# A four-layer graph network: tables stored from 128 partitions, POOL's gathers written out, and the first half chunk taken ahead of the fill

## The chip, the cores and the metric

The kernel runs on one core of a Trainium2 chip. Its time is the device time of one execution in microseconds; several runs were made, and their median counts. The trace comes from one further execution under the hardware profiler. Engines go by the profile's names: PE (TensorE), DVE (VectorE), ACT (ScalarE), POOL (GpSimd), SP (SyncE, which here only starts DMAs).

## What is computed

A graph with N = 3125 nodes of 32 features and E = 53125 edges, sorted by destination node (every node has at least its loop). Four layers follow one another, each as `x = layernorm(x + layer(x))`. Cut to what matters:

```python
# layer 0: GAT with 4 heads, then a GRU cell on its sum
e = leaky_relu(el[src] + er[dst], 0.2)
alpha = softmax over the edges of one dst (e)
agg = segment_sum(feat[src] * alpha, dst)          # feat: N x 4 x 32
# layer 1: Chebyshev convolution of order 3 (two sums over edges), then GATv2
agg = segment_sum((x * Dinv)[src], dst)            # twice: cheb0, cheb1
e = leaky_relu(fsrc[src] + fdst[dst], 0.2); logits = e . attn; softmax; segment_sum
# layer 2: spline convolution, 4 x 4 tent basis of two edge attributes
msg = sum_k basis[:, k] * (x[src] @ w2[k]); out = segment_sum(msg, dst)
# layer 3: AGNN
alpha = beta * (x_norm[dst] . x_norm[src]); softmax; segment_sum(w * x[src], dst)
```

## The kernel before

**Layout.** Edges lie on 125 partitions (`NP`), 425 in a row (`T`); nodes lie on 125 partitions, 25 (`J`) each. `P` is 128, `SLOT` is 16, what a finished DMA adds to its semaphore, and `LS` is 5.

**Passes.** Five passes run over the edges: gat, cheb0, cheb1, gatv2 and agnn. Each takes the 425 columns in 17 chunks (`CH`) of 25 (`L`), in two buffers of `rows`. Every chunk needs the source node's row for each edge. Of its 25 columns, TensorE fetches 12 (gat) or 14 (`PE_COLS`) from a table that it holds, by products with one-hot matrices (L740); for that SP loads the source numbers to every partition (`load_sources`, L475), VectorE makes the one-hots (L1099), ScalarE the last of them (L921), and VectorE takes the products from PSUM with predicated copies (`take_half`, L1125). The other 13 or 11 columns POOL gathers by indirect DMA from a table in DRAM (`gather`, L600), which SP stored at the stage's start (`store_table`, L443). For each chunk SP loads the 25 columns of indices into `idx`; POOL waits for them and for the buffer (`rows_used`), adds two columns of ones into `fence` (L622, a `tensor_tensor` whose end the next fence waits for) and issues the gathers. VectorE then makes logits, running maxima and segmented scans, SP stores each scanned chunk, and at a pass's end POOL gathers 25 columns of node sums.

**Order on VectorE at a pass's start.** `begin_pass` (L1306) makes the parts of the table for TensorE and the one-hots of two chunks. Softmax passes then call `fill_edges` (L1293): it waits for the destination rows that were scattered into `starts_dram` and loaded back to `edges_d`, and spreads them over the edges with scans (64 in gatv2 and agnn, 8 in gat). `softmax_pass` (L1350) begins with three memsets (`start_scans`) and `take_half(0, 0, 0)`, which frees a part of PSUM for TensorE's next products.

**The spline stage.** TensorE multiplies each node's features with the weights (L879), ScalarE copies the products into `staged` in the layout of `tab_y` (L1040), five node columns a group, in two buffers, and SP stores each group of five columns as one DMA (L526): five stores of 2812 KB. ScalarE waits before group g for store g - 2. After the first store SP also stores the cell numbers that VectorE makes (L531), and loads them piece by piece into `idx` (L538), behind all stores of `tab_y`. POOL waits for the stores and the indices and gathers for each of 85 slots five rows of 128 floats (L600), in five buffers; from the sixth slot on there is a fence (L686) before each slot. VectorE works on each slot (L1696 to L1718), TensorE sums it (L785).

**What sets the order.** The orders on the engines are written out by hand. The helper `chunks` (L300) runs a pass's steps as two steps, a loop of 6 turns of two steps, and 3 steps; POOL's program uses it and a second loop for the spline, as SP's does.

## Time and profile before

| | before |
|---|---|
| runs | 2799.86, 2793.50, 2805.55 us; median 2799.86 |
| profiled execution | 2798.72 us |
| its span, first to last instruction | 2797.0 us |
| busy: PE, DVE, POOL, ACT | 69%, 64%, 68%, 31% of the span |
| mean granted TensorE clock | 0.831 of full |
| passes: POOL's first instruction to the end of its last row gather | gat 94.2 to 445.7, cheb0 579.9 to 843.7, cheb1 907.2 to 1170.0, gatv2 1271.3 to 1594.8, agnn 2430.9 to 2729.8 |
| spline: tab_y stored 1653.7 to 1766, gathers 1766.8 to 2368.8 | |

Busy shares are means over stages that differ. The times of the passes tell in which stage an instruction of a given start time lies. The profiled execution's time is 1.7 us longer than its span.

### The profile page before, as it was taken

Reading aid. Unit: us, or ns where it says so; the run is one execution under the profiler, and the core shown is the slowest. Engines: PE = TensorE matmul, PEld = TensorE weight load, DVE = VectorE, ACT = ScalarE, POOL = GpSimd, SP = SyncE. Lnnn points to the kernel's source line nnn. Section 1 sums busy time; section 2 is a strip of 40 time slices with the busy share of each in tenths; the row PEclk is TensorE's granted clock in tenths of the full one; section 3 lists DMA queues with packets and bytes.
Section 4 is the critical chain, followed back from the end, with each engine's and each line's share of the span. In section 5 each row is a group of like instructions: output and inputs, shape, how many; then the busy total and the mean of one; then the engine's idle time right before and its main releaser. Section 6 shows DMA issues by size and latency. Waiting matters only on the chain.

```text
span 2797.0 us, 52360 instructions
## 1 busy us (share of the span) xinstructions
PE 1938.7 (69%) x19915; PEld 1682.9 (60%) x19915; DVE 1784.3 (64%) x4803; ACT 879.6 (31%) x804; POOL 1915.2 (68%) x1825
## 2 busy tenths in 40 slices
PE   2577773669990999643988633487877788359990
PEld 2577773469990999633988611354544455259990
DVE  7499996155551455426878740477777777488785
ACT  0376774134440455310544322000000000125442
POOL 6788883357774777657888630588888887547873
PEclk6789886579995999856999855799999999679995
DMA  6243342123221322113222113211211111323321
GB/s 218 51 130 106 104 130 81 26 53 73 66 61 32 64 66 67 47 34 121 62 61 61 41 55 135 67 46 46 47 46 46 47 46 42 128 49 65 72 55 26
DMA packets 104646, 194.01 MB, mean 69 GB/s; under 512 B 52441, under 2 KB 71713, under 8 KB 100983
## 3 DMA queue, kind: packets, MB, share of 16 engines
q1 hardware_dynamic: 51528, 137.86, 13.3%
q0 software_dynamic: 53024, 54.88, 12.6%
q8 instruction: 62, 1.02, 0.2%
q14 instruction: 32, 0.26, 0.0%
HBM read 107.45 MB, written 85.19 MB: 69 GB/s over the span
## 4 chain that ended last, share of the span: by engine, by line
POOL 26%; issue 13%; DVE 10%; PE 10%; DMA 8%; ACT 1%; POOLq 0%; DVEq 0%; SPq 0%
POOL edges_d L600 16%; PE ps L740 8%; POOL rows L600 7%; DVE edges_d L1302 2%; DMA tab_y_dram<-edges_d 2%; POOL starts_dram L603 1%; POOL agg L600 1%; DMA idx<-cell_dram 1%; POOL fence L686 1%; DMA edges_d<-starts_dram 1%; DMA rows<-tab_fsrc_dram,idx 1%; PE ps L879 1%; DMA rows<-tab_x_dram,idx 1%; DVE bigT L1388 0%; DVE rows L1125 0%
## 5 line engine op out<-in xcount | busy, mean ns | idle before, releaser
L600 POOL DMA_INDIRECT edges_d<-tab_y_dram,idx x425 | 451.6, 1063 | 230.3 <-DMA idx<-cell_dram 113.6
L740 PE MATMUL ps<-nodes,edges_d 125*128 125x160 bf16 x7140 | 499.9, 234 | 101.9 <-ACT edges_d L921 98.4
L740 PEld LDWEIGHTS ps<-nodes,edges_d 125*128 125x128 bf16 x7140 | 498.4, 98 | 103.4 <-ACT edges_d L921 101.0
L785 PE MATMUL ps<-edges_d,scan 125*125 125x480 bf16 x1700 | 388.7, 390 | 142.2 <-DVE edges_d L1718 142.2
L600 POOL DMA_INDIRECT rows<-tab_cheb_dram,idx x374 | 407.0, 1088 | 109.1 <-issue 106.8
L740 PE MATMUL ps<-nodes,aggn 125*128 125x180 bf16 (+2 forms) x3372 | 377.9, 245 | 145.1 <-DVE rows L1125 145.1
L740 PE MATMUL ps<-nodes,agg 125*128 125x180 bf16 (+2 forms) x3564 | 342.6, 246 | 145.6 <-ACT aggn L921 80.7
L785 PEld LDWEIGHTS ps<-edges_d,scan 125*125 125x125 bf16 x1700 | 241.7, 145 | 289.7 <-DVE edges_d L1718 113.9
L1125 DVE COPY_PREDICATED rows<-picks,ps 125x192 f32<-125x192 uint16 (+4 forms) x850 | 342.7, 404 | 75.9 <-PE ps L740 23.3
L740 PEld LDWEIGHTS ps<-nodes,agg 125*128 125x128 bf16 x3564 | 290.1, 102 | 150.3 <-ACT aggn L921 81.4
L740 PEld LDWEIGHTS ps<-nodes,aggn 125*128 125x128 bf16 x3372 | 280.7, 102 | 149.5 <-issue 105.4
L600 POOL DMA_INDIRECT rows<-tab_dram,idx x221 | 272.9, 1235 | 64.7 <-issue 59.1
L600 POOL DMA_INDIRECT rows<-tab_fsrc_dram,idx x187 | 257.6, 1377 | 54.7 <-issue 52.4
L600 POOL DMA_INDIRECT rows<-tab_x_dram,idx x187 | 212.2, 1135 | 55.0 <-issue 52.4
L1696 DVE TENSOR_TENSOR edges_d<-edges_d 125x640 f32<-125x640 f32 x85 | 70.2, 826 | 247.1 <-DMA edges_d<-tab_y_dram,idx 247.1
L1049 ACT ACTIVATE agg<-prod 125x160 bf16<-125x160 f32 x85 | 28.6, 337 | 612.8 <-DVE prod L1707 612.8
L740 PE MATMUL ps<-nodes,smallT 125*128 125x160 bf16 (+1 forms) x2016 | 182.3, 236 | 0.0
L944 ACT ACTIVATE bigT<-rows 125x800 f32<-125x800 f32 x34 | 56.2, 1653 | 308.6 <-DVE rows L1125 308.6
L740 PEld LDWEIGHTS ps<-nodes,smallT 125*128 125x128 bf16 x2016 | 151.8, 99 | 0.0
L972 ACT ACTIVATE bigT<-rows 125x800 f32<-125x800 f32 x34 | 54.2, 1595 | 277.6 <-DVE idle L1475 151.0
L1692 DVE TENSOR_SCALAR scan<-nodes,codes 125x625 bf16<-125x625 f16 x340 | 133.1, 408 | 0.0
L603 POOL DMA_INDIRECT starts_dram<-scat,start_i x75 | 76.5, 1019 | 81.4 <-DVE scat L1760 28.1
(330 smaller groups left out, 3123.9 us busy)
## 6 DMA issues: line engine op xcount, KB each, us to landing
src<-srcT_dram SPq DMA_DIRECT2D x68, 427.2 KB
scan_dram<-scan SPq DMA_DIRECT2D x17, 1700.0 KB
scan_dram<-scan SPq DMA_DIRECT2D x34, 425.0 KB
tab_y_dram<-edges_d SPq DMA_DIRECT2D x5, 2812.5 KB
scanD_dram<-scan SPq DMA_DIRECT2D x34, 400.0 KB
edges_d<-starts_dram SPq DMA_DIRECT2D x2, 3408.0 KB, 20.1
starts_dram<-scan SPq DMA_DIRECT2D x2, 3400.0 KB, 15.3
edges_d<-tab_y_dram,idx POOLq DMA_INDIRECT x425, 2.6
```

The costliest lines, as they stand in the source:

```text
L600: pool.indirect_dma_start(o, None, table, bass.IndirectOffsetOnAxis(index, 0)).then_inc(s, SLOT)
L603: pool.indirect_dma_start(table, bass.IndirectOffsetOnAxis(index, 0), rows_, None, bounds_check=last, oob_is_err=False).then_inc(scattered ...
L686: pool.tensor_tensor(fence[:, 0:1], ones[:, 0:1], ones[:, 1:2], ALU.add)\
L740: ins = pe.matmul(columns_ps[:, i, 0:PICKS * w], hots_[b][lot][:, i * NP:i * NP + P], parts_[:, part, at:at + PICKS * w], start=(lot == 0 ...
L785: ins = pe.matmul(ps[0:NP, lot, 0:PICKS * 3 * D], lot_hots[c][:, t, lot, :], picked[c][:, t, :, :].rearrange("p k c -> p (k c)"), start=(b ...
L944: nc.scalar.activation(z[b][:, at:at + D, :], r[:, :, 0:D].rearrange("p t f -> p f t"), ACT.Copy).then_inc(rows_flipped, 1)
L972: nc.scalar.activation(z[b], rows[0:NP, b, 0:L * D].rearrange("p (t c) -> p c t", c=D), ACT.Copy).then_inc(rows_used, 1)
L1049: nc.scalar.activation(parts[:, c, :, 0:D], prod[:, c * LS:(c + 1) * LS, :], ACT.Copy)\
L1125: ins = vec.copy_predicated(to[:, cols[0]:cols[-1] + 1, 0:w], over(picks[:, b, pick, cols[0]:cols[-1] + 1], w), columns_ps[0:NP, cols[0]:c ...
L1302: ins = vec.tensor_tensor_scan(ed[:, t0:t1, c], same[:, t0:t1], ed[:, t0:t1, c], ed[:, t0 - 1, c:c + 1] if i else 0.0, ALU.mult, ALU.add)
L1692: vec.tensor_scalar(lot_hots[c][:, t, :, :].rearrange("p l c -> p (l c)"), nodes16[:, 0:LOTS * NP], codes[:, c, t:t + 1], None, ALU.is_equal)
L1696: vec.tensor_tensor(slot, slot, over(basis[:, bass.ds(t0 + c * LS, LS), :], D), ALU.mult)\
```

## The change

DRAM tables get 128 × 25 rows in place of 3125, and every table store, the stores of `tab_y` and the loads of source numbers go from or to 128 partitions instead of 125. POOL's program has no loops any more; the fences and their semaphore are gone; the indices are no longer loaded chunk by chunk: all source numbers lie in `src_i`, loaded once at the start, and the cell numbers in `cell_i`, where VectorE writes them. `fill_edges` is called inside `softmax_pass`, behind the first `take_half`. Three memsets clear partitions 96 to 127 of the buffers.

```diff
-        tab_cheb_dram = [dram("tab_cheb0_dram", (N, D)), dram("tab_cheb1_dram", (N, D))]
-        tab_y_dram = dram("tab_y_dram", (N * CELLS * CELLS, CORNERS * D))
-        cell_dram = dram("cell_dram", (E,), I32)
+        tab_cheb_dram = [dram("tab_cheb0_dram", (P * J, D)), dram("tab_cheb1_dram", (P * J, D))]
+        tab_y_dram = dram("tab_y_dram", (P * J * CELLS * CELLS, CORNERS * D))
...
-        idx = sb("idx", [P, 2, L], I32)
+        src_i = sb("src_i", [P, T], I32)
...
-        attr = sb("attr", [NP, T, 2])
+        attr = sb("attr", [P, T, 2])
+        cell_i = attr[:, :, :].rearrange("p t d -> p (t d)")[:, 0:T].bitcast(I32)
...
-        staged = edges_d[0:NP, 0:2 * LS * YROW].rearrange("p (b j c) -> p b j c", b=2, j=LS)
+        staged = edges_d[:, 0:2 * LS * YROW].rearrange("p (b j c) -> p b j c", b=2, j=LS)
...
+                    if a is lambda_max_row:
+                        sp.wait_ge(tails_cleared, 1)
+                        sp.dma_start(src_i[0:NP, :], src_grid).then_inc(src_loaded, SLOT)
...
-                        sp.dma_start(src16[0:NP, b, 0:n * NP], srcT_dram[bass.ds(t0 + L - n, n), :]
-                                     .rearrange("t p -> (t p)").partition_broadcast(NP)).then_inc(src16_in[b], SLOT)
+                        sp.dma_start(src16[:, b, 0:n * NP], srcT_dram[bass.ds(t0 + L - n, n), :]
+                                     .rearrange("t p -> (t p)").partition_broadcast(P)).then_inc(src16_in[b], SLOT)
 
                     def step(k, b, t0):
-                        if gathered[b].n or k >= 2:
-                            sp.wait_ge(rows_in[b], gathered[b].at())
-                        sp.dma_start(idx[0:NP, b, :], src_grid[:, bass.ds(t0, L)]).then_inc(idx_in[b], SLOT)
-                        gathered[b].up(SLOT * (L - PE_COLS[name]))
                         if k < CH - 1:
                             load_sources(k + 1, 1 - b, t0 + L)
...
-                store_table(tab_cheb_dram[0], tabf[0:NP, 0:J * D])
+                store_table(tab_cheb_dram[0], tabf[:, 0:J * D])
...
-                    if g == 0:
-                        sp.wait_ge(cells_made, 1)
-                        sp.dma_start(cell_grid, cell_i).then_inc(cells_stored, SLOT)
-                sp.wait_ge(cells_stored, SLOT)
...
-                load_indices(0, True)
-                with sp.Fori(0, CH - 1) as turn:
-                    for c in slot_n:
-                        c.enter(turn, SLOT * LS)
-                    load_indices(turn * L + L, False)
...
-                    def step(k, b, t0):
-                        pool.wait_ge(idx_in[b], loaded[b].up(SLOT))
+                    for k in range(CH):
                         if k >= 2:
                             pool.wait_ge(rows_used, used.up())
-
-                        if fences.n:
-                            pool.wait_ge(fence_done, fences.at())
-                        pool.tensor_tensor(fence[:, b:b + 1], ones[:, 0:1], ones[:, 1:2], ALU.add)\
-                            .then_inc(fence_done, 1)
-                        fences.up()
                         for t in range(L - PE_COLS[name]):
-                            gather(rows[:, b, t * width:(t + 1) * width], table, idx[:, b, t:t + 1], rows_in[b])
-
-                    chunks(pool, [(loaded[0], SLOT), (loaded[1], SLOT), (used, 2), (fences, 2)], step)
+                            gather(rows[:, k % 2, t * width:(t + 1) * width], table,
+                                   src_i[:, k * L + t:k * L + t + 1], rows_in[k % 2])
...
-                for c in range(SLOTS):
-                    pool.wait_ge(slot_idx_in[c], idx_n[c].up(SLOT))
-                    gather_slot(c)
-                with pool.Fori(0, CH - 1) as turn:
...
+                pool.wait_ge(cells_made, 1)
+                for n in range(CH * SLOTS):
+                    if n >= SLOTS:
+                        pool.wait_ge(slot_used, n - SLOTS + 1)
                     for t in range(LS):
-                        gather(slots[:, c, t * CORNERS * D:(t + 1) * CORNERS * D], tab_y_dram,
-                               idx[:, 0, c * LS + t:c * LS + t + 1], slot_in[c])
+                        gather(slots[:, n % SLOTS, t * CORNERS * D:(t + 1) * CORNERS * D], tab_y_dram,
+                               cell_i[:, n * LS + t:n * LS + t + 1], slot_in[n % SLOTS])
...
+                vec.memset(src_i[96:P, :].bitcast(F32), 0.0)
+                vec.memset(attr[96:P, :, :], 0.0).then_inc(tails_cleared, 1)
+                vec.memset(tab[96:P, :, :], 0.0)
...
-                def softmax_pass(name, logits):
+                def softmax_pass(name, logits, fill_width, fill_at):
                     table, width, scan_dram, C, heads = PASSES[name]
                     z, keep, n = scan_views(name)
                     start_scans(name)
                     take_half(0, 0, 0, name)
+                    fill_edges(fill_width, fill_at)
...
                 begin_pass("gat", tab[0:NP, :, 0:D + H], 1)
-                fill_edges(H, D + H)
```

Three places of the engines' orders follow; a row is a line of the kernel, the operation, the written and read names and the shape, with what it waits for.

On VectorE, at the start of gatv2, before (`edges_d` holds the destination rows, `picks` and `ps` belong to `take_half`; the scans are named SCALAR_TENSOR_TENSOR here):

```order
L1109 TENSOR_SCALAR picks<-pick_of 125x70
L1299 COPY edges_d<-first_row 125x32
L1302 SCALAR_TENSOR_TENSOR edges_d<-same,edges_d 125x212 x32
L1302 SCALAR_TENSOR_TENSOR edges_d<-same,edges_d 125x213 x32
L1334 MEMSET bigT 125x33
L1335 MEMSET bigT 125x33
L1336 MEMSET mrun 125x4
L1124 MEMSET idle 125x1
L1125 COPY_PREDICATED rows<-picks,ps 125x192
```

and after the change (its line numbers are those of the changed kernel):

```order
L1054 TENSOR_SCALAR picks<-pick_of 125x70
L1282 MEMSET bigT 125x33
L1283 MEMSET bigT 125x33
L1284 MEMSET mrun 125x4
L1069 MEMSET idle 125x1
L1070 COPY_PREDICATED rows<-picks,ps 125x192
...
L1070 COPY_PREDICATED rows<-picks,ps 125x192
L1247 COPY edges_d<-first_row 125x32
L1250 SCALAR_TENSOR_TENSOR edges_d<-same,edges_d 125x212 x32
L1250 SCALAR_TENSOR_TENSOR edges_d<-same,edges_d 125x213 x32
```

The copies of the first half chunk (five instructions, of which the first and the last stand here; the second half's stay behind) and the memsets now come ahead of the 65 instructions of the fill.

On POOL, in the spline stage, before (the end of the first slots, the loop's entry and its first slot):

```order
L600 DMA edges_d<-tab_y_dram,idx 128x128 [waits slot_idx_in3]
L600 DMA edges_d<-tab_y_dram,idx 128x128 x4
L600 DMA edges_d<-tab_y_dram,idx 128x128 [waits slot_idx_in4]
L600 DMA edges_d<-tab_y_dram,idx 128x128 x4
L677 UNCONDITIONAL_BRANCH
L677 ISA
L684 ISA [waits slot_idx_in0]
L685 REGISTER_ALU [waits slot_used]
L686 TENSOR_TENSOR fence<-ones 128x1 [waits fence_done]
L600 DMA edges_d<-tab_y_dram,idx 128x128 x5
```

and after:

```order
L628 IOTA nodes 125x625
L573 DMA edges_d<-tab_y_dram,attr 128x128 [waits cells_made,products_stored1,products_stored0]
L573 DMA edges_d<-tab_y_dram,attr 128x128 x24
L573 DMA edges_d<-tab_y_dram,attr 128x128 [waits slot_used]
L573 DMA edges_d<-tab_y_dram,attr 128x128 x4
L573 DMA edges_d<-tab_y_dram,attr 128x128 [waits slot_used]
L573 DMA edges_d<-tab_y_dram,attr 128x128 x4
```

The branch, the fences and the waits for index loads are gone; the wait for `slot_used` stands at each slot's first gather, and `attr` is the memory that holds the cell numbers.

On SP, around the stores of `tab_y`, before:

```order
L526 DMA tab_y_dram<-edges_d 125x5760 [waits group_copied]
L531 DMA cell_dram<-aggn 125x425 [waits cells_made]
L526 DMA tab_y_dram<-edges_d 125x5760 [waits group_copied] x4
L538 DMA idx<-cell_dram 125x5 [waits cells_stored]
L538 DMA idx<-cell_dram 125x5 x4
```

and after:

```order
L473 DMA src<-srcT_dram 128x1750 [waits last_hot_ready]
L486 DMA scan_dram<-scan 128x850 [waits rows_turned] x4
L520 DMA tab_y_dram<-edges_d 128x5760 [waits group_copied] x5
L441 DMA tab_x_dram<-tab 128x825 [waits vec_for_sync]
L441 DMA tab_xn_dram<-scat 128x800 [waits vec_for_sync]
```

The store and the loads of the cell numbers are gone, and the five stores come from 128 partitions.

## Rows read from the trace of the kernel before

**Rows 1.** The page: span, busy time and its share by engine

```profile
span 2797.0 us, 52360 instructions
PE 1938.7 (69%) x19915; PEld 1682.9 (60%) x19915; DVE 1784.3 (64%) x4803; ACT 879.6 (31%) x804; POOL 1915.2 (68%) x1825
```

**Rows 2.** Stretches: length, busy us by engine (PE to POOL), clock, DMA share, GB/s

```profile
58.00:72.00 14.00, 0.58 (x2) 0.49 (x2) 11.79 (x29) 0.22 (x1) 8.41 (x8) 0.50 1.02 423
570.00:579.00 9.00, 0.00 (x0) 0.00 (x0) 2.91 (x4) 0.00 (x0) 0.00 (x0) 0.50 0.32 96
1733.00:1764.00 31.00, 0.00 (x0) 0.00 (x0) 0.00 (x0) 0.00 (x0) 0.00 (x0) 0.50 0.32 136
1766.00:2370.00 604.00, 474.32 (x2082) 296.29 (x2083) 444.52 (x1040) 28.28 (x84) 483.97 (x505) 0.92 0.19 47
```

**Rows 3.** Chain that ended last, 1640 to 1790: start, us, what

```profile
1653.70 25.08 DMA tab_y_dram<-edges_d
1688.37 34.87 DMA tab_y_dram<-edges_d
1731.91 34.08 DMA idx<-cell_dram
```

**Rows 4.** ACT's timeline, spline stage: start, us, instruction [idle before, releaser]

```profile
1663.38 1.32 ACT L1040 ACTIVATE edges_d<-ps 125x288 f32<-125x288 f32 x4 [0.39 <-PE ps L879]
1678.80 2.53 ACT L1040 ACTIVATE edges_d<-ps 125x288 f32<-125x288 f32 x8 [14.10 <-DMA tab_y_dram<-edges_d]
```

**Rows 5.** Line L459, two stores of 3400 KB: their landing

```profile
DMA to landing us min/median/max: 11.2/15.3/19.4
```

**Rows 6.** Spline: two groups of the page, then two lines' instructions

```profile
L600 POOL DMA_INDIRECT edges_d<-tab_y_dram,idx x425 | 451.6, 1063 | 230.3 <-DMA idx<-cell_dram 113.6
L1696 DVE TENSOR_TENSOR edges_d<-edges_d 125x640 f32<-125x640 f32 x85 | 70.2, 826 | 247.1 <-DMA edges_d<-tab_y_dram,idx 247.1
...
L600 POOL DMA_INDIRECT edges_d<-tab_y_dram,idx x425: 940/964/1587, 1766.8 to 2367.7; - x142
...
L686 POOL TENSOR_TENSOR fence<-ones x80: 200/400/662, 1800.6 to 2361.2; 128x1 f32<-128x1 f32 x80
```

**Rows 7.** POOL's timeline inside the spline stage, around two fences

```profile
1998.82 1.14 POOL L600 DMA_INDIRECT edges_d<-tab_y_dram,idx  x1 [0.30 <-issue]
1999.98 0.20 POOL L686 TENSOR_TENSOR fence<-ones 128x1 f32<-128x1 f32 x1
2000.33 0.96 POOL L600 DMA_INDIRECT edges_d<-tab_y_dram,idx  x1 [0.15 <-issue]
...
2006.54 0.59 POOL L686 TENSOR_TENSOR fence<-ones 128x1 f32<-128x1 f32 x1
```

**Rows 8.** Timelines at the Chebyshev passes (SP, DVE, POOL, ACT, POOL)

```profile
568.38 0.28 SPq L443 DMA_DIRECT2D tab_cheb_dram<-tab  x1
579.69 2.53 DVE L1099 TENSOR_SCALAR edges_d<-src,lot_f 125x1754 bf16<-125x1754 f16 x4 [6.67 <-DMA src<-srcT_dram]
579.92 0.49 POOL L622 TENSOR_TENSOR fence<-ones 128x1 f32<-128x1 f32 x1 [56.21 <-issue]
845.13 1.54 ACT L972 ACTIVATE bigT<-rows 125x800 f32<-125x800 f32 x1 [7.88 <-DMA rows<-tab_cheb_dram,idx]
907.15 0.50 POOL L622 TENSOR_TENSOR fence<-ones 128x1 f32<-128x1 f32 x1 [16.40 <-issue]
```

**Rows 9.** Timelines at gatv2 and agnn, and the page's group L1125

```profile
1282.67 0.18 DVE L1299 COPY edges_d<-first_row 125x32 f32<-125x32 f32 x1 [23.70 <-DMA edges_d<-starts_dram]
1319.14 0.56 PE L740 MATMUL ps<-nodes,aggn 125*128 125x160 bf16 x3 [43.82 <-DVE rows L1125]
1329.69 0.19 POOL L622 TENSOR_TENSOR fence<-ones 128x1 f32<-128x1 f32 x1 [6.18 <-DVE bigT L1388]
2488.67 0.19 POOL L622 TENSOR_TENSOR fence<-ones 128x1 f32<-128x1 f32 x1 [25.49 <-DVE bigT L1388]
L1125 DVE COPY_PREDICATED rows<-picks,ps 125x192 f32<-125x192 uint16 (+4 forms) x850 | 342.7, 404 | 75.9 <-PE ps L740 23.3
```

91 lines of the change are left out of this document (28 added, 63 removed).

## The prediction

> **What bounds the kernel now.** I read the page first. No engine fills the span: TensorE is busy 69%, VectorE 64%, POOL 68% [rows 1], so the stages have different limits, and a change is worth what the last wait of its stage is worth. Then I read the chain of work that ended last, to find stretches in which no engine works. The largest lies between the second layer's attention pass (gatv2) and the third layer's spline convolution: two stores of the table tab_y, 25.08 and 34.87 us, and then an index load that takes 34.08 us [rows 3]. That load is small; it stands behind the last tab_y store in SP's queue. POOL's first spline gather starts at 1766.8 and had waited 113.6 us for it [rows 6].
>
> In the Chebyshev passes the start is late: the table is stored at 568.38, VectorE gets its source numbers at 579.69 after idling 6.67, POOL starts at 579.92, and the last chunk still waits 7.88 us for gathered rows [rows 8]. So POOL's stream, shifted by its late start, ends last there.
>
> In gatv2 and agnn VectorE fills the rows of the destination table (64 scans, some 34 us) before it takes the first half chunk, and TensorE stands 43.82 us until then [rows 9]. Afterwards POOL's stream is again what the others wait for, so TensorE's idle time is worth little.
>
> **The change, part by part.**
>
> *tab_y stores.* Before, store 0 goes at 1653.70 and lands at 1678.78. ScalarE, which writes the staging buffers, waits 14.10 us for it at the third group [rows 4], and so once for each later group. A store of 128 partitions moves 2880 KB; at 423 GB/s that is 6.8 us. What lies around the transfer I take from the starts stores: 3400 KB are 8.0 us at that rate and the first lands after 11.2 [rows 5], so 3.2 us are added: 10.0 us a store. ScalarE makes a group of five tiles in 9.57 us (1678.80 to 1688.37) [rows 3, 4]; a store of 10.0 us is back before its buffer is wanted, two groups later. So ScalarE no longer waits. It ended the second group at 1663.38 + 1.32 = 1664.70 [rows 4], and three groups later stands at about 1694.5 (two of them hold an extra copy, so about 9.9 each). The last store lands at 1704.5 and the first gather comes 0.7 later, about 1705, for 1766.8 before: **−61.8 us**. VectorE has nothing to do in the stretch from 1733 [rows 2], so the cell numbers that POOL's gathers also need are no bound. Bounds: if ScalarE's groups come at 7.2 us (its own busy time), −69; if a store needs 17 us because several buffers, other queues or the memory slow it, −55.
>
> *The fence in the spline.* 80 fences of 400 ns median go [rows 6]. What one costs POOL is its spacing against that of two gathers. In the quiet case the gather ends at 1999.96, the fence runs 0.20 and the next gather starts at 2000.33: 0.37 between the ends where 0.30 is normal [rows 7], so 0.07 each, 5.6 us in all. From the sums: 424 spacings take 600.9 us (1766.8 to 2367.7), a plain spacing is 1.063 + 0.30 = 1.363 [rows 6, 7], 344 of them are 468.9, and the 80 with a fence come to 1.65 each: 0.287 more, 23 us in all. The difference between the ends is that half of the fences are stretched to 0.59 to 0.66 beside VectorE's work [rows 7]. Whether that stretching goes with them or falls on the gathers is open; a gather is stretched too (0.96 to 1.14). I take **−12**, near the middle, with 5.6 and 23 as ends. POOL stays the bound: of 604 us TensorE is busy 474.3 and VectorE 444.5 [rows 2], 5.6 and 5.2 us of the 7.07 per slot.
>
> The Trainium skill bears on this ("SBUF — State Buffer", on the port pair that VectorE and GpSimd share): the pair is locked for a whole instruction, and a gather's descriptors cannot be written until VectorE's operation ends. By that rule the stretching belongs to VectorE's operations and not to the fence, the gathers would inherit it, and the sum would be smaller by about 6 us. The stretched fence of 0.59 beside one of 0.20 agrees with a lock; no row here shows who inherits it.
>
> *Chebyshev passes.* The table store of 400 KB needs about 1 us of transfer at 423 GB/s and the 3.2 us around it, so POOL may start at about 572.3 in place of 579.9; its first fence and the step behind it (0.64) go, and 15 fences at 0.07. That is 7.6 + 0.6 + 1.0 = 9.2 on POOL's side. On VectorE's side the idle 6.67 vanishes, since the 427 KB of source numbers (1 us at 423 GB/s, behind 1 us of table, and the 3.2) land at about 573.6 where VectorE came free at 573.0, 6.67 before 579.69; the second load, 1 us behind, is then hidden too. POOL's rows end last by the 7.88 [rows 8]; when POOL gains 9.2 and VectorE about 7, the wait shrinks and POOL still ends last. **−9** for cheb0, and **−9** for cheb1, whose first fence stands in the same way at 907.15 after 16.40 idle [rows 8]. Ends −6.5 and −10 each.
>
> *The fill behind the first half chunk.* In gatv2 the five predicated copies of the half chunk (5 × 0.404 [rows 9], 2.0) and three small memsets (0.2, an estimate) move from behind the fill into idle time ahead of it, since VectorE waits there 23.70 us for the destination rows [rows 9]. POOL waits 6.18 us for chunk 0 to be used, so it gains those 2.2, and 15 × 0.07 for fences: **−3.3**. In agnn POOL waits 25.49 [rows 9]: the same 2.2, 1.1 of fences, and, an estimate, 1.3 of a shorter wait of POOL on chunk 1: **−4.6**. TensorE's 43.8 us idle are filled with chunk 1's products, which nobody waited for. If POOL were not the bound behind it, chunk 1's second half would be worth up to 5 us in each; if the fill's scans find TensorE's results no earlier, nothing.
>
> *gat* I leave almost as it is: **−0.4**, its 17 fences at 0.07 (1.2) a third on the path (0 to −3).
>
> *The start.* Three memsets are added on VectorE ahead of its wait for the destination numbers: **+0.2** (0 to 1). The load of all source numbers (212 KB) stands ahead of some weights and is hidden by the gathers of destination rows that VectorE waits for afterwards; if it is not hidden it costs 212 KB at the 136 GB/s of five engines [rows 2], 1.6.
>
> *Indices.* 170 small index loads go, with their issue time on SP and their latency; in the steady stream they were early, so nothing beyond the above.
>
> *Sum.* −61.8 − 12 − 9 − 9 − 3.3 − 4.6 − 0.4 + 0.2 = −99.9. The profiled span of 2797.0 becomes 2697.1, the profiled execution's 2798.7 becomes 2698.8. The median of the runs shown is 1.1 above the profiled execution, so I say **2699 us**.
>
> **The rivals.** About 0.5% (14 us) is what a measurement of this kernel can tell from no change.
>
> *Contention stays and moves (0.15).* The wider loads of source numbers (one per chunk, 16 engines for 1 us in place of five for 3) and the bare stream of gathers are stretched more: every plain spacing in the spline goes up by 0.09 to 1.45, as in the slowest stretches. Then the spline saves 5.6 and loses 38; total about −62 or 2737. For it: plain gathers range from 0.94 to 1.59 [rows 6]. Against: the extremes are few (median 0.964).
>
> *The wide store does not spread (0.04).* If tab_y and the other tables still go over five engines, only the fences, the order of SP's queue (no index load behind the last store is needed, but POOL waits for the store itself) and the fill are left: −12 − 2 − 2 − 3.3 − 4.6, about −24: 2775. Against: stores and loads of 128 partitions on the same queue show share 1.02.
>
> *More than forecast (0.18).* ScalarE's groups come faster, because TensorE, busy without gaps, is granted a higher clock than 0.50 in that stretch (windows: 0.50 while it idles), and the fences' full 23 us come back: −69 − 23 − 10 − 10 − 6 − 6 = −124, or 2675.
>
> *Slower (0.03).* POOL's program is now written out: 1394 gathers in a row where a loop of one turn's length stood. If fetching them cost POOL 0.08 us or more a gather ((100 + 14) / 1394), the gain would be gone; at 0.12 the time is 2866. Against: a turn of the spline loop already holds 25 gathers in a straight run, and they go at 0.94 + 0.30 at their quickest [rows 6, 7], which is the issue time of any gather here. The Trainium skill ("Runtime: NRT & Kernel Launch", section "Instruction fetch mechanics") says that crossing a fetched block is mostly hidden and that a taken branch is what stalls; by that rule the change gains a little there.
>
> *The forecast* itself has 0.6.
>
> **How the numbers follow.** The forecast's own range adds its ends: −69 − 23 − 13 for the best (2684 to 2690 if not all at once) and −55 − 5.6 − 13 − 5 for the worst (2720): 2682 to 2720. Eight in ten: down to 2670, which takes in the larger gain, and up to 2726, which takes in a part of the contention case; the rest of it, the unspread store and the slower case are left out. Faster by over 0.5% in all cases but the slower one and mishaps between: 0.96; same 0.015; slower 0.025.
>
> **What the profile after would show.** Windows of a lone tab_y store with a share near 1.0 and above 400 GB/s; ScalarE without waits on tab_y in the spline stage; first spline gather near 1705 less what the stages ahead gained (about 22 us), so near 1683; gather spacing 1.36 or less and a slot of 6.9 us; POOL's first cheb0 gather 4 us behind the table store; TensorE without the 43.8 us in gatv2 and agnn. The prediction is wrong if the tab_y stores take over 15 us each, if gathers stretch beyond 1.4 spacing, or if POOL shows gaps between gathers above 0.30 that nothing releases.

## The result, and the profile after

The changed kernel takes 2660.85 us (median of four runs, 2658.53 to 2662.79) against 2800.41 (2793.50 to 2805.55). The ratio is 0.9503, 95% interval 0.9481 to 0.9525: 139.6 us less. The forecast was 2699, and its range ended at 2670. The profiled execution took 2661.16, its span is 2658.2, which is 138.8 less than that of [rows 1].

The page of the changed kernel, with the groups that answer to [rows 6] (gathers are line L573 here, and L1643 is what was L1696):

```profile
span 2658.2 us, 51172 instructions
PE 1904.6 (72%) x19915; PEld 1661.4 (63%) x19915; DVE 1801.5 (68%) x4806; ACT 879.6 (33%) x804; POOL 1846.9 (69%) x1659
...
L573 POOL DMA_INDIRECT edges_d<-tab_y_dram,attr x425 | 431.9, 1016 | 180.7 <-issue 129.2
...
L1643 DVE TENSOR_TENSOR edges_d<-edges_d 125x640 f32<-125x640 f32 x85 | 71.2, 837 | 131.1 <-DMA edges_d<-tab_y_dram,attr 131.1
```

The gathers of the spline take 1016 ns on average where they took 1063, VectorE waits for them 131.1 us where it waited 247.1, and the fences' group is gone.

I cut the two traces at POOL's gathers, whose first start and last end mark each stage. "Sums" are the 25 gathers of node sums that follow each pass. Times in us; the last column is how far the changed kernel had pulled ahead by the event, and in brackets what the stage itself added.

| event | before | after | ahead by (stage) |
|---|---|---|---|
| sums of gat begin | 491.6 | 489.0 | 2.6 (2.6) |
| sums of cheb0 begin | 859.8 | 850.0 | 9.8 (7.2) |
| sums of cheb1 begin | 1186.0 | 1171.3 | 14.7 (4.9) |
| sums of gatv2 begin | 1621.4 | 1594.2 | 27.2 (12.5) |
| first spline gather | 1766.8 | 1677.5 | 89.3 (62.1) |
| last spline gather ends | 2368.8 | 2238.5 | 130.3 (41.0) |
| sums of agnn begin | 2754.6 | 2615.7 | 138.9 (8.6) |

The stores of tab_y gave what was forecast (62.1 for 61.8). The spline stage gave 41.0 where 12 were forecast, gatv2 12.5 for 3.3, agnn 8.6 for 4.6, the Chebyshev passes together 12.1 for 18, and all ahead of them 2.6 for 0.2.

Two stretches of the changed kernel (columns as in [rows 2]): around the cheb0 table store, and while a tab_y store is under way.

```profile
565.00:572.00 7.00, 0.00 (x0) 0.00 (x0) 6.46 (x9) 0.00 (x0) 2.73 (x3) 0.50 0.68 191
1660.00:1666.00 6.00, 6.00 (x8) 1.82 (x7) 0.00 (x0) 4.14 (x13) 0.00 (x0) 0.50 1.01 430
```

The tab_y store now has a DMA share of 1.01 and 430 GB/s, where it had 0.32 and 136 [rows 2]. Its five stores land after (line L520):

```profile
DMA to landing us min/median/max: 8.2/8.2/8.7
```

That is 8.2 us a store; I had worked out 10.0. ScalarE's timeline in the same stage, and POOL's first spline gather:

```profile
1657.04 1.32 ACT L985 ACTIVATE edges_d<-ps 125x288 f32<-125x288 f32 x4 [0.39 <-PE ps L824]
1667.64 1.32 ACT L985 ACTIVATE edges_d<-ps 125x288 f32<-125x288 f32 x4 [0.51 <-PE ps L824]
...
1677.45 0.96 POOL L573 DMA_INDIRECT edges_d<-tab_y_dram,attr  x1 [51.52 <-DMA tab_y_dram<-edges_d]
```

ScalarE's waits on tab_y [rows 4] are gone; it waits 0.39 to 0.51 for TensorE's products, and now and then 1.7 to 2.2. POOL begins 8.5 us after ScalarE's last copy ends (1668.96), one landing and the issue.

POOL's timeline inside the spline stage, one slot of five gathers and the next slot's first:

```profile
1904.25 0.94 POOL L573 DMA_INDIRECT edges_d<-tab_y_dram,attr  x1 [0.30 <-issue]
1905.50 1.25 POOL L573 DMA_INDIRECT edges_d<-tab_y_dram,attr  x1 [0.30 <-issue]
1907.05 0.94 POOL L573 DMA_INDIRECT edges_d<-tab_y_dram,attr  x1 [0.30 <-issue]
1908.30 0.94 POOL L573 DMA_INDIRECT edges_d<-tab_y_dram,attr  x1 [0.30 <-issue]
1909.55 1.08 POOL L573 DMA_INDIRECT edges_d<-tab_y_dram,attr  x1 [0.30 <-issue]
1910.94 0.94 POOL L573 DMA_INDIRECT edges_d<-tab_y_dram,attr  x1 [0.30 <-issue]
```

This slot takes 6.69 us (1904.25 to 1910.94). Three of its gathers are unstretched, one takes 1.25 and one 1.08. The stage has 85 slots in 561 us, 6.6 each, for 7.07 before.

The start of cheb0 (SP's table store, POOL's first gather, TensorE's first product, POOL's first gather of chunk 2):

```profile
565.75 0.33 SPq L441 DMA_DIRECT2D tab_cheb_dram<-tab  x1
...
568.66 0.94 POOL L573 DMA_INDIRECT rows<-tab_cheb_dram,src_i  x1 [47.65 <-DMA tab_cheb_dram<-tab]
...
577.01 23.17 PE L685 MATMUL ps<-nodes,edges_d 125*128 125x160 bf16 x298 [31.29 <-ACT edges_d L866]
...
600.59 0.94 POOL L573 DMA_INDIRECT rows<-tab_cheb_dram,src_i  x1 [4.18 <-ACT bigT L917]
```

POOL starts 2.9 us after the store, where it had taken 11.5 [rows 8]. But then it waits 4.18 us at chunk 2 for a buffer. TensorE starts 11.3 us after the store, where it took 17.4 in the trace before, whose store goes at 568.38 [rows 8]:

```profile
585.76 26.42 PE L740 MATMUL ps<-nodes,edges_d 125*128 125x160 bf16 x347 [37.41 <-ACT edges_d L921]
```

The fill in gatv2 (VectorE's copy and scans, TensorE's wait behind it, POOL's gathers beside it):

```profile
1267.88 0.29 DVE L1247 COPY edges_d<-first_row 125x32 f32<-125x32 f32 x1 [24.46 <-DMA edges_d<-starts_dram]
1268.20 11.96 DVE L1250 TENSOR_TENSOR_SCAN edges_d<-same,edges_d 125x212 f32<-125x212 f32 x24
...
1306.43 0.58 PE L685 MATMUL ps<-nodes,aggn 125*128 125x160 bf16 x3 [50.64 <-DVE rows L1070]
...
1275.83 9.09 POOL L573 DMA_INDIRECT rows<-tab_fsrc_dram,src_i  x1 [0.30 <-issue]
1288.14 14.65 POOL L573 DMA_INDIRECT rows<-tab_fsrc_dram,src_i  x1 [0.31 <-issue]
...
1313.11 0.96 POOL L573 DMA_INDIRECT rows<-tab_fsrc_dram,src_i  x1 [3.71 <-DVE bigT L1337]
```

TensorE still stands 50.64 us, for 43.82 before [rows 9], and two of POOL's gathers take 9.09 and 14.65 us while the scans run (9.10 and 14.66 in the trace before).

### The profile page after: what moved, and what is told of

Its sections match the earlier page's. It is cut to its first block, busy times and chain, and to the rows that moved or that the text cites. A ratio compares the mean times of both kernels' runs of the same rounds, so it can differ in the third digit from the quotient of the medians.

```text
span 2658.2 us, 51172 instructions
## 1 busy us (share of the span) xinstructions
PE 1904.6 (72%) x19915; PEld 1661.4 (63%) x19915; DVE 1801.5 (68%) x4806; ACT 879.6 (33%) x804; POOL 1846.9 (69%) x1659
## 4 chain that ended last, share of the span: by engine, by line
POOL 37%; issue 13%; DVE 7%; PE 4%; DMA 3%; ACT 1%; POOLq 0%; DVEq 0%; ACTq 0%
POOL rows L573 19%; POOL edges_d L573 16%; DVE edges_d L1250 2%; PE ps L685 2%; PE ps L824 2%; POOL starts_dram L576 1%; POOL agg L573 1%; DMA edges_d<-starts_dram 1%; DMA tab_y_dram<-edges_d 0%; ACT edges_d L985 0%; DVE bigT L1293 0%; PE ps L809 0%; PE ps L805 0%; PE ps L730 0%; DMA local<-scan_dram,mend_get_i 0%
## 5 line engine op out<-in xcount | busy, mean ns | idle before, releaser
L573 POOL DMA_INDIRECT edges_d<-tab_y_dram,attr x425 | 431.9, 1016 | 180.7 <-issue 129.2
L573 POOL DMA_INDIRECT rows<-tab_cheb_dram,src_i x374 | 409.7, 1095 | 177.4 <-issue 112.5
L730 PE MATMUL ps<-edges_d,scan 125*125 125x480 bf16 x1700 | 364.1, 371 | 108.6 <-DVE edges_d L1665 108.6
L685 PE MATMUL ps<-nodes,agg 125*128 125x180 bf16 (+2 forms) x3564 | 337.3, 244 | 112.9 <-ACT aggn L866 58.6
L730 PEld LDWEIGHTS ps<-edges_d,scan 125*125 125x125 bf16 x1700 | 227.9, 137 | 245.9 <-DVE edges_d L1665 113.0
L573 POOL DMA_INDIRECT rows<-tab_dram,src_i x221 | 277.0, 1253 | 67.5 <-issue 66.4
L573 POOL DMA_INDIRECT rows<-tab_fsrc_dram,src_i x187 | 250.5, 1340 | 60.4 <-issue 56.7
L573 POOL DMA_INDIRECT rows<-tab_x_dram,src_i x187 | 228.3, 1221 | 61.9 <-issue 56.7
L1069 DVE MEMSET idle<- 125x1 f32 x850 | 50.1, 59 | 171.6 <-PE ps L685 129.9
L1643 DVE TENSOR_TENSOR edges_d<-edges_d 125x640 f32<-125x640 f32 x85 | 71.2, 837 | 131.1 <-DMA edges_d<-tab_y_dram,attr 131.1
L889 ACT ACTIVATE bigT<-rows 125x800 f32<-125x800 f32 x34 | 56.3, 1656 | 310.4 <-DVE rows L1070 310.4
L917 ACT ACTIVATE bigT<-rows 125x800 f32<-125x800 f32 x34 | 54.2, 1595 | 277.3 <-DVE idle L1424 151.6
L1639 DVE TENSOR_SCALAR scan<-nodes,codes 125x625 bf16<-125x625 f16 x340 | 142.9, 437 | 0.0
```

What stands on the lines that cost most here:

```text
L573: pool.indirect_dma_start(o, None, table, bass.IndirectOffsetOnAxis(index, 0)).then_inc(s, SLOT)
L685: ins = pe.matmul(columns_ps[:, i, 0:PICKS * w], hots_[b][lot][:, i * NP:i * NP + P], parts_[:, part, at:at + PICKS * w], start=(lot == 0 ...
L730: ins = pe.matmul(ps[0:NP, lot, 0:PICKS * 3 * D], lot_hots[c][:, t, lot, :], picked[c][:, t, :, :].rearrange("p k c -> p (k c)"), start=(b ...
L889: nc.scalar.activation(z[b][:, at:at + D, :], r[:, :, 0:D].rearrange("p t f -> p f t"), ACT.Copy).then_inc(rows_flipped, 1)
L917: nc.scalar.activation(z[b], rows[0:NP, b, 0:L * D].rearrange("p (t c) -> p c t", c=D), ACT.Copy).then_inc(rows_used, 1)
L1069: vec.memset(idle[:, half * 8 + pick:half * 8 + pick + 1], 0.0)
```

## The experiments

All are against the changed kernel (2660.9 us), but for the first two, which are the kernel before with parts of the change. Given are medians and the ratio to the kernel before, measured beside each on the same chip (2797.5 to 2804.6 us). Lengths of stages come from the one profiled execution of each kernel and not from the median (in e3 and e9 it was the quickest of four). A pass's stream is POOL's first row gather to the end of its last.

### Which part gives what

**e1_tables.** The kernel before, and all table stores from 128 partitions:

```diff
-                store_table(tab_cheb_dram[0], tabf[0:NP, 0:J * D])
+                store_table(tab_cheb_dram[0], tabf[:, 0:J * D])
...
-        staged = edges_d[0:NP, 0:2 * LS * YROW].rearrange("p (b j c) -> p b j c", b=2, j=LS)
+        staged = edges_d[:, 0:2 * LS * YROW].rearrange("p (b j c) -> p b j c", b=2, j=LS)
```

> The kernel before with one part of the change: all table stores, those of tab_y too, from 128 partitions. Source numbers, indices, fences, loops and the fill's place are as before. If the stores alone give what the trace of after suggests, the wait for tab_y falls by 62 us and the two Chebyshev passes start 8 us earlier each on POOL's side, of which the narrow load of source numbers takes back some: together 62 to 78 us, a time of 2722 to 2738. If the wide store gains only together with the removal of the cell index load, the gain stays under 40 us.

2733.69 us, ratio 0.9743 (0.9723 to 0.9762): 71 less. Its first spline gather stands at 1702.8, so the wide store alone is worth the tab_y term; the removal of the cell index load isn't needed for it.

**e2_no_pool.** As e1, with the wide loads of source numbers and the fill behind the first half chunk; POOL's program as before.

> The change without its POOL part: wide stores, wide loads of source numbers and the fill behind the first half chunk are in; loops, fences and index loads stay as before. Theory (fences, or what comes with them, cost far more than 0.07 us each): 2715 to 2730, so that POOL's part is worth 55 to 70 us, and a spline slot stays at 7.07 us. Rival (wide loads or the stores relieve the gathers): the spline stage is already shorter here, a slot is at 6.6 us, and the time is under 2700.

2721.97 us, 0.9714 (0.9697 to 0.9730). The spline stage takes 600.4 us, as before (602.1). So the spline's gain, and 61 us in all, come with POOL's part (fences, loops and index loads).

**e5_narrow_src.** Source numbers loaded to 125 partitions again:

```diff
-                        sp.dma_start(src16[:, b, 0:n * NP], srcT_dram[bass.ds(t0 + L - n, n), :]
-                                     .rearrange("t p -> (t p)").partition_broadcast(P)).then_inc(src16_in[b], SLOT)
+                        sp.dma_start(src16[0:NP, b, 0:n * NP], srcT_dram[bass.ds(t0 + L - n, n), :]
+                                     .rearrange("t p -> (t p)").partition_broadcast(NP)).then_inc(src16_in[b], SLOT)
```

> The changed kernel with the source numbers loaded to 125 partitions, as before. Theory (in the Chebyshev passes TensorE, not POOL, sets the end once POOL starts early, so that what counts there is when the first source numbers land): 2.5 us more in each Chebyshev pass and 2 us more ahead of gat, 7 to 8 us in all, 2668 to 2670. Rival (POOL's stream still ends last): no change in the two passes, 2661 to 2664. Second rival (the wide loads stretch the gathers of the other passes): the time falls.

2672.75 us, 0.9553 (0.9531 to 0.9576), 12 more, above every range of the expectation. In the trace cheb0 and cheb1 are longer by 3.2 us each, with POOL's start as early as in the changed kernel (569.2 and 568.7). TensorE's first product comes at 579.24 for 577.01. The rest are short waits of TensorE of 0.3 to 0.9 us. In cheb0 TensorE takes 252.5 us from its first product to the last of the 17 chunks, 251.2 in the changed kernel and 252.1 in the kernel before, whenever POOL started. So the passes' end follows TensorE, and not POOL. The two passes hold 6.4 of the 12 us; of the others 3.1 lie in the spline, whose instructions are the same, and 1.9 in gatv2. The 2 us ahead of gat did not come (sums of gat at 489.3 for 489.0).

### What the fences cost

**e3_spline_fence.** The 80 fences of the spline put back into the straight program:

```diff
                         pool.wait_ge(slot_used, n - SLOTS + 1)
+                        if fences.n:
+                            pool.wait_ge(fence_done, fences.at())
+                        pool.tensor_tensor(fence[:, 0:1], ones[:, 0:1], ones[:, 1:2], ALU.add).then_inc(fence_done, 1)
+                        fences.up()
```

> The changed kernel with the 80 fences of the spline stage put back; no index loads, no loops. Theory (the fence is what made a slot 7.07 us): the spline stage grows by 35 to 41 us and the time is 2696 to 2702. Rival (the index loads and the loop did it): a fence adds only its quiet cost of 0.07 to 0.3 us, 6 to 23 us in all, and the time is 2667 to 2684.

2707.07 us, 0.9662 (0.9639 to 0.9685): 46 more, and in the trace the spline stage is 601.6 us, 40.6 longer, 0.51 a fence. Its loops and index loads are gone, and the stage is as long as before: with the fences in place they cost nothing there. The size has a margin: the stage takes 600.4 to 602.1 in five traces with 80 fences, and 561.0 to 571.3 in eight without a POOL operation in their places, so 80 fences cost 29 to 41 us. POOL's timeline, two fences a slot apart, with VectorE's L1672 ahead of each:

```profile
1903.36 1.41 DVE L1672 TENSOR_TENSOR edges_d<-agg,pick_bits 125x1200 int32<-125x1200 int32 x1
1905.60 0.21 POOL L641 TENSOR_TENSOR fence<-ones 128x1 f32<-128x1 f32 x1
1905.96 0.96 POOL L576 DMA_INDIRECT edges_d<-tab_y_dram,attr  x1 [0.15 <-POOL fence L641]
...
1911.32 1.41 DVE L1672 TENSOR_TENSOR edges_d<-agg,pick_bits 125x1200 int32<-125x1200 int32 x1
1912.19 0.60 POOL L641 TENSOR_TENSOR fence<-ones 128x1 f32<-128x1 f32 x1
1912.93 0.97 POOL L576 DMA_INDIRECT edges_d<-tab_y_dram,attr  x1
1914.21 1.40 POOL L576 DMA_INDIRECT edges_d<-tab_y_dram,attr  x1 [0.30 <-issue]
```

The pattern is that of [rows 7]: a fence of 0.21, and one of 0.60 with a gather of 1.40 behind it. The trace says which are stretched. All 40 stretched fences (0.59 and more) start while VectorE runs L1672, an operation of 1.41 us that reads two operands from SBUF, and end 0.05 us after it; all 40 short ones start while VectorE is idle. In the trace before it is the same, 40 and 40, with L1718.

**e8_two_fences.** Two fences at each of those places.

> The changed kernel with two fences at each place of the spline stage. Theory A (each fence has a price of its own, 0.5 us): the stage grows by another 35 to 41 us against one fence, about 642 us, and the time is 2740. Theory B (a slot of POOL's stream and VectorE's work on it lock into a pattern, and the first fence moved them into a worse one): the second fence costs its quiet 0.2 to 0.35 us a slot, 16 to 28 us, or the stage is even shorter than with one; 600 to 628 us.

2743.33 us, 0.9801 (0.9781 to 0.9821); the stage takes 640.0 us, 38.4 more than with one. A second fence costs as much as the first, and theory B falls. But the price is not the stretching of the fences themselves: 159 of these 160 take their short 0.2 us and start while VectorE is idle, and all 160 together take 32.5 us, as the 80 did (32.4). The further 38.4 us are on the gathers, whose mean rises from 1062 to 1138 ns, and in the gaps between. Why the gathers pay for it when the fences don't, no run here takes apart.

**e7_spline_memset** and **e11_one_operand.** In the fences' places a memset, and a copy:

```diff
+                        pool.memset(fence[:, 0:1], 1.0).then_inc(fence_done, 1)
...
+                        pool.tensor_copy(fence[:, 0:1], ones[:, 0:1]).then_inc(fence_done, 1)
```

> The changed kernel with a memset of one column on POOL in each place where the spline stage had a fence: an operation of the same place and semaphore that reads nothing. The 80 fences put back made the stage 40.6 us longer. Theory 1 (any POOL operation between gathers costs this, since it must wait for the memory port that VectorE holds, and delays the gathers behind it): 35 to 41 us more than the changed kernel, about 2700. Theory 2 (it is the reading of two operands from the memory): 5 to 15 us more, 2666 to 2676.

> The changed kernel with a copy of one column (one operand read from the memory, one written) in each place where the spline stage had a fence. The fence, which reads two operands, cost 40.6 us there, and a memset, which reads none, 9.0. If it is the second operand that makes the fence wait for VectorE's port: about 9 to 14 us, 2670 to 2675. If any reading costs it: 30 to 41 us, 2691 to 2702.

The memset: 2673.08 us, 0.9552 (0.9534 to 0.9569), stage 570.0, 9 us more than in the changed kernel, but within the 561.0 to 571.3 of the kernels with nothing there: a cost of its own isn't shown. The copy: 2695.27 us, 0.9642 (0.9624 to 0.9661), stage 600.4, 39.4 more, all but the fence's price. POOL's timelines, the memset first, with VectorE's L1672 ahead of it:

```profile
1901.29 1.41 DVE L1672 TENSOR_TENSOR edges_d<-agg,pick_bits 125x1200 int32<-125x1200 int32 x1
1902.14 0.11 POOL L641 MEMSET fence<- 128x1 f32 x1
1902.44 1.08 POOL L576 DMA_INDIRECT edges_d<-tab_y_dram,attr  x1 [0.19 <-POOL fence L641]
```

```profile
1905.32 0.20 POOL L641 COPY fence<-ones 128x1 f32<-128x1 f32 x1
1905.68 0.98 POOL L576 DMA_INDIRECT edges_d<-tab_y_dram,attr  x1 [0.15 <-POOL fence L641]
...
1911.85 0.60 POOL L641 COPY fence<-ones 128x1 f32<-128x1 f32 x1
1912.61 0.98 POOL L576 DMA_INDIRECT edges_d<-tab_y_dram,attr  x1 [0.16 <-POOL fence L641]
1913.90 1.43 POOL L576 DMA_INDIRECT edges_d<-tab_y_dram,attr  x1 [0.30 <-issue]
```

The memset is never stretched (80 of them take 118 ns on average, 125 at most), though 68 of the 80 start inside L1672. The copy alternates between 0.20 and 0.60 with a stretched gather behind the latter, just as the fence does; its 41 stretched ones all start inside L1672. So it isn't the second operand, and not any operation either. What is stretched is a POOL operation that reads SBUF while VectorE runs a two-operand operation. That the reading does it, and nothing else in which a memset differs from a copy, rests on these three operations.

**e6_pass_fence** and **e13_all_fences.** The 85 fences of the passes put back, and all 165.

> The changed kernel with the 85 fences of the five passes put back. Theory (a fence costs POOL 0.5 us where VectorE is dense and POOL's stream sets the end, and nothing where TensorE does): gatv2 7 to 9 us, agnn 2 to 5, gat 0 to 2, the Chebyshev passes 0; 10 to 15 us more, 2671 to 2676. Rival (loops and index loads were the cost of these passes): under 4 us more.

> The changed kernel with all 165 fences put back, its program still without loops and index loads. Theory (fences are all of POOL's part): 2718 to 2724, as the kernel with everything but POOL's part (2722). Rival (loops and index loads have a share of their own): 2705 or less.

e6: 2682.78 us, 0.9574 (0.9555 to 0.9593), 22 more. Chunks 2 to 16 take 262.1 us in gatv2 for 254.7, and 245.0 in agnn for 235.7; gat's stream is 10.3 longer without moving its sums (489.2), and the Chebyshev passes get no longer. Against the expectation agnn lost more than gatv2, and 10 us lie in the spline, whose code was not touched (below). e13: 2709.16 us, 0.9679 (0.9660 to 0.9699), 48 more, between the two expectations. There the same chunks take 257.7 and 239.7. Only agnn's difference is clear of what the same code does by itself: its stream takes 298.8 (e6) and 295.8 (e13) with fences and 289.3 to 293.1 in six kernels whose agnn has none, so its 17 fences cost 2.7 to 9.5 us. gatv2's takes 318.1 and 313.8 with fences, and 308.7 to 323.1 in the same six: a price of the fences there isn't shown. Nor do the parts add up, 46 (e3) and 22 (e6) against 48 for both. e13 stays 13 us below e2. Of POOL's 61 us fences are 48. The spans of e13 and e2 differ by only 7.0 us, of which 6.2 lie between the sums of cheb1 and of gatv2 and 2.5 in agnn's stage; whether that is the loops, the index loads or the scatter shown by e12 below was not told apart. The kernel before without fences wasn't run.

### The fill

**e4_fill_first.** The fill ahead of the first half chunk again:

```diff
+                    fill_edges(fill_width, fill_at)
...
                     take_half(0, 0, 0, name)
-                    fill_edges(fill_width, fill_at)
```

> The changed kernel with the fill of destination rows ahead of the first half chunk again, as before, in the three softmax passes. Theory (the place of the fill is worth the 2.2 us of the moved copies in gatv2 and agnn each, and the rest of the gain of these passes is the fences'): 3 to 7 us more, 2664 to 2668. Rival (TensorE's 43.8 idle us matter later in the pass): 12 us or more.

2672.99 us, 0.9531 (0.9515 to 0.9547): 12 more, the rival's number. From POOL's first gather to that of chunk 2 gatv2 takes 57.9 us for 55.9, and agnn 56.3 for 54.2: the moved copies' 2.0 us, as forecast. The rest lies in the chunks behind (259.4 for 254.7, 240.2 for 235.7) and in the spline (565.1 for 561.0), where the instructions are the same. In gatv2 and the spline that is within what the same code does by itself (e12); agnn's stream, 296.5, is not (289.3 to 293.1), so the rival isn't excluded there. Nor is the 2.0 seen everywhere: between e1 and e2, which move the fill with the fences in place, gatv2's falls from 58.8 to 56.3 while agnn's stays (58.5 and 58.6).

**e12_same_again.** The changed kernel once more, for how far a stage of the same code repeats.

> The changed kernel itself once more. If the lengths of gatv2, spline and agnn are properties of the code, they come out as in its first profile, 310.6, 561.0 and 289.9 us from POOL's first row gather to the end of the last, within 1 us, and the median at 2659 to 2663. If they depend on how the two engines happen to lock into each other, they differ by several us (the same code took 308.8 to 323.1 for gatv2 in the kernels with changed neighbours).

2663.11 us, 0.9519 (0.9506 to 0.9532). gatv2 took 312.3 us for 310.6, spline 564.5 for 561.0, agnn 289.3 for 289.9. So a stage repeats within 3.5 us in the same kernel, and from kernel to kernel the untouched spline took 561.0 to 571.3, the untouched stream of gatv2 308.7 to 323.1 (e8, where only the spline differs) and that of agnn 289.3 to 293.1. Differences of a stage within these ranges are no evidence, gatv2's least of all.

**e9_split_fill.** The fill cut at column 50, the second part after chunk 1:

```diff
-        FILLS = [(0, T // 2), (T // 2, T)]
+        FILLS = [(0, 2 * L), (2 * L, T)]
...
-                                 (kept, 2), (used, 2), (flipped, 2), (scanned, 2)] + HOT_COUNTS, step)
+                                 (kept, 2), (used, 2), (flipped, 2), (scanned, 2)] + HOT_COUNTS, step,
+                           lambda: fill_edges(fill_width, fill_at, 1))
```

> The changed kernel, and the fill cut in two at column 50 in place of 212: the first 50 columns are loaded and filled ahead of chunk 0, the other 375 after chunk 1. In gatv2 and agnn VectorE can begin chunk 0 some 34 us earlier (the load of 50 columns lands about 6 us earlier and 28 us of scans come later). Theory (POOL waits for chunk 0 to be used and is then the bound, VectorE idles 25 us a pass in all): 15 to 30 us less per pass, 2600 to 2630. Rival (VectorE becomes the bound at once, or gathers blocked beside the fill eat it): only the earlier load of 6 us a pass, 2645 to 2652.

2676.25 us, 0.9556 (0.9535 to 0.9577), 15 more, where 9 to 61 less were expected. VectorE did begin chunk 0 early, and POOL's chunk 2 begins 34.9 us after its first gather for 55.9. But beside the second part of the fill POOL loses it again:

```profile
1313.03 1.46 POOL L573 DMA_INDIRECT rows<-tab_fsrc_dram,src_i  x1 [0.30 <-issue]
1314.79 22.00 POOL L573 DMA_INDIRECT rows<-tab_fsrc_dram,src_i  x1 [0.30 <-issue]
1337.10 1.49 POOL L573 DMA_INDIRECT rows<-tab_fsrc_dram,src_i  x1 [0.30 <-issue]
```

One gather takes 22.00 us. POOL reaches chunk 4 of gatv2 92.0 us after its first gather, for 90.2 in the changed kernel, where the fill blocked two gathers for 23.7 together and POOL waited only 3.71 more. Ahead of chunk 0 that blocking costs nothing: in e11, with the same gatv2, no gather beside the fill took over 1.3, and chunk 2 began after 55.7 us for 55.9. Behind chunk 1 it falls into time in which POOL has buffers to fill. Where the 15 us are isn't shown by this: in the profiled execution gatv2's whole stage is 3.6 us shorter, agnn's 5.7 longer, and 7.8 lie in the untouched spline.

**e10_uneven_fill.** `FILLS = [(0, 130), (130, T)]`, all of it ahead of chunk 0.

> The changed kernel with the fill's two loads cut at column 130 in place of 212, all of it still ahead of chunk 0. The first load is 3.2 us shorter, so the fill starts and ends 3.2 us earlier, and POOL waits 3.7 and 5.2 us for chunk 0 in gatv2 and agnn. Theory: 3 us less in each, 2654 to 2656. Rival (a slot or chunk pattern of VectorE and POOL swallows or doubles such shifts, as between kernels with the same code in these stages, whose gatv2 took 307.7 to 315.6 us): anything from 2648 to 2670, and the gain at the second fill's end is seen while the pass's end is not earlier.

2654.63 us, 0.9491 (0.9474 to 0.9508), 6.2 and 8.5 less than the two measurements of the changed kernel. VectorE's scans in gatv2, and POOL's first gather of chunk 2:

```profile
1262.09 10.47 DVE L1250 TENSOR_TENSOR_SCAN edges_d<-same,edges_d 125x130 f32<-125x130 f32 x32
1273.57 23.32 DVE L1250 TENSOR_TENSOR_SCAN edges_d<-same,edges_d 125x295 f32<-125x295 f32 x32 [1.00 <-DMA edges_d<-starts_dram]
...
1308.01 0.97 POOL L573 DMA_INDIRECT rows<-tab_fsrc_dram,src_i  x1 [2.46 <-DVE bigT L1337]
```

The second part waits 1.00 us for its rows, so the two loads and the scans are near balance at 130; no other cut was run. Chunk 2 begins 53.9 us after the first gather for 55.9, and in agnn 51.6 for 54.2. Of this agnn keeps nothing: its chunks behind take 238.4 for 235.7, and the stream ends after 290.0 for 289.9, which was the expectation's rival. In the trace gat gave 1.7 us and gatv2's stage 2.4, the latter within its scatter.

**e14_best.** e10 with the last store of tab_y in two parts, three node columns and then two.

> The changed kernel with the fill's loads cut at column 130 (which gave 6 to 8 us) and the last store of tab_y cut in two, three node columns and then two, so that after the last product only 1152 KB are to be stored: 2.7 us at the rate of the wide stores in place of 6.8, the first three columns being under way before. If the last store's landing is what POOL's first spline gather waits for: 3 to 4 us less than with the cut fill alone, 2649 to 2652. If the stores queue up behind each other, no gain: 2653 to 2656.

2654.85 us (2643.99 to 2658.69), 0.9484 (0.9464 to 0.9505). POOL's first spline gather comes 5.1 us after ScalarE's last copy for 8.5, so the stage gained the 3.4; the total doesn't show it beyond its spread. Its fill is that of e10, and yet chunk 2 begins 58.0 and 56.1 us after the first gather for 53.9 and 51.6, with gathers of 10.05 and 18.57 us beside gatv2's scans; the agnn stream still takes only 288.8. So the start of chunk 2 does not by itself set a pass's end. Both medians lie 6 us or more below those of the changed kernel (2660.85 and 2663.11); between the two nothing is decided.

## Why the prediction was wrong

**The step that failed** is *the fence in the spline*, and with it the fences in agnn. I bounded it by 0.07 us (a quiet fence) and by 0.287, the sum's excess at fences over a plain spacing, and took −12 of at most −23. It is 40.6 for 80 fences (e3; 29 to 41 by the other traces), and again 38.4 for a second set (e8). The upper bound was no bound: I took the plain spacing of the kernel with fences as what a gather costs anyway, 1.363. Part of that stretching came with the fences. Without them a spacing is 1.32, so 344 plain spacings gave back some 15 us beside what the 80 gave. A price read as "spacing with, less spacing without" must take the "without" from a stretch that has none; the trace before had such stretches only in other stages.

The other reading of that part, that the stretching belongs to VectorE's operations and the gathers would inherit it and make the gain smaller, fell too: the gain was larger, and the plain spacings shrank with the fences gone. The prediction told the lock without its condition. The Trainium skill ("SBUF — State Buffer", section "Who interferes with whom") says that a VectorE instruction with two SBUF inputs contends with a GpSimd instruction that reads SBUF, and not with one that only writes it. The traces agree: beside the two-input L1672 all fences and copies that started inside it were stretched to its end plus 0.04 to 0.05 us, and 68 memsets took their 0.12 or less. Had I applied the condition, it would have told which operation to put in the fence's place, though not the price.

*The fences in the passes*, 0.07 each, were the same mistake in agnn, where 17 of them cost 2.7 to 9.5 us (e6, e13) where the sum has 1.1; that is enough for agnn's −8.6 in place of −4.6. For gatv2's −12.5 against −3.3 no cause is shown: with fences put back its stage is 6.8 (e6) and 2.5 (e13) longer, and 11.9 longer in e8, which leaves it untouched. In gat and the Chebyshev passes they cost nothing, though gat's stream of gathers shrank by 7 us, because POOL doesn't set the end there.

*tab_y stores* were right in mechanism and size: −62.1 for −61.8, and e1 shows that the width alone does it. That it is right to 0.3 us is luck: landing and issue of the last store took 8.5 us for my 10.7, and ScalarE ended its last group 42.6 us after the first store where I had 40.8.

*Chebyshev passes*: right in sign, wrong in what ends last. I let POOL's 9.2 us decide because the last chunk waited for gathered rows. POOL did start 8.6 us sooner after the store, and then waited 4.18 for a buffer, since the consumers are paced by TensorE, which runs with no pause over 0.7 us from its first product to its last (e5 delays TensorE alone, and both passes grow by 3 us). The passes gained 7.2 and 4.9, of which TensorE's start explains 6.1 in cheb0.

*The fill*: the 2.0 us at chunk 0 are seen in both passes of e4 and in gatv2 from e1 to e2, and not in agnn there; that they reach a pass's end isn't shown. That TensorE's 43.8 idle us would be filled was wrong: it made the half chunk that the freed part of PSUM allows, and then stood 50.64 us. It cost nothing, as forecast.

*gat and the start*: 2.6 for 0.2. From e1 to e2 the sums of gat come 2.3 us earlier (492.0 and 489.7), which points to the wide loads of source numbers; e5 didn't take it back, so this stays open.

*The rivals.* "More than forecast" had −124 with 0.18 of the chances and the right direction, but by the wrong route: TensorE's clock stayed at 0.50 in the tab_y stage, though it was busy for 42.8 of the 48 us from 1620 to 1668, and the fences gave 40.6, not 23. Contention did not rise, the store did spread, and no gather showed a gap of fetching: the issue gaps are 0.30 as before. The range ended at 2670, since I cut it at the fences' false bound. Two sums of the prediction are wrong by its own terms, and neither made the miss: −69 − 23 − 13 gives about 2694 and not 2684 to 2690, and the contention case (−99.9 with 5.6 in place of 12, plus 38) gives −55.5 or 2743, not 2737.

## What to carry to other kernels

## What was not expected of the hardware

A POOL memset of one column (118 ns) was never stretched beside VectorE in 80 places, 68 of them inside the two-operand L1672, while a copy or sum of one column took 0.20 us when VectorE was idle and 0.60 when it started inside that operation, ending 0.04 to 0.05 us after it. A second such sum cost as much as the first (38.4 and 40.6 us for 80), though only one of the 160 was stretched. Beside the 64 back-to-back scans of a fill (33.8 us) most gathers took 1.18 us for 0.94, but in some traces one or two were held far longer (9.09 and 14.65; 22.00 when the scans were longer), across many scans, and in others with the same code none was (e11). And stages whose instructions are the same differed by up to 10 us of 561 (spline) and 14 of 309 (gatv2's stream) between kernels, with 3.5 between two executions of one.
